# A gated attention and ternary feed-forward block: attention first in a step, exponentials last, work moved from VectorE to ScalarE and GpSimd

## The reference

```python
x = x + jnp.tanh(g_xattn[0]) * _L0_xattn_ref(_layernorm(x, axis=-1), ctx_1024, ctx_1024, ...)
x = x + jnp.tanh(g_ffn[0]) * _L0_ffn_ref(_layernorm(x, axis=-1), w_gate, w_up, w_down)
# one head of the attention: ig, fg are gates of the token, from q, k and v
cs = concatenate([0, cumsum(log_sigmoid(fg))])
log_D = where(lower_triangle, (cs - cs.T)[1:, 1:], -inf) + ig.T
D = exp(log_D - max_log_D)
C = (q @ (k.T / sqrt(DH))) * D
h = C / (maximum(abs(C.sum(-1)), exp(-max_log_D)) + EPS) @ v      # then an RMS norm per head
# the feed-forward half: activations rounded to 8 bits per token, weights to -1, 0, 1
g = act_quant(x) @ weight_quant(w_gate).T
u = act_quant(x) @ weight_quant(w_up).T
h = square(relu(g)) * u
out = act_quant(h) @ weight_quant(w_down).T
```

## Time and profile before

| | |
|---|---|
| median of 3 runs | 704.64 us (703.66 to 706.67) |
| the profiled execution | 707.75 us, of it the span of the core 706.0 us |
| TensorE busy | 602.2 us (85%), granted clock 0.944 of full speed on average |
| VectorE busy | 568.5 us (81%) |
| ScalarE busy | 424.0 us (60%) |
| GpSimd busy | 97.9 us (14%) |
| HBM traffic | 63.73 MB, mean 90 GB/s |

### The profile page before, as it was taken

How to read it: one execution, slowest core, us unless ns; L and a number is a source line. 1 busy time by engine, 2 the same in 40 slices (tenths; PEclk the granted TensorE clock), 3 DMA queues, 4 the chain that set the end, 5 groups by cost and what they waited for, 6 DMA issues and landing times.

```text
span 706.0 us, 18248 instructions
## 1 busy us (share of the span) xinstructions
PE 602.2 (85%) x6596; PEld 347.4 (49%) x6596; DVE 568.5 (81%) x1288; ACT 424.0 (60%) x893; POOL 97.9 (14%) x170
## 2 busy tenths in 40 slices
PE   7384776989989898998989898989989898989887
PEld 4151433545545454554646454555546464556443
DVE  4388559797879879697988979797979889797965
ACT  4376894657466465757556565657466565666542
POOL 1165020101001010101001010101000010101000
PEclk9797888999999999999999999999999999999999
DMA  9945201304040220404040230405040311402000
GB/s 311 381 160 177 85 0 56 127 17 165 3 165 15 97 82 15 164 0 164 15 164 15 64 116 15 164 0 179 0 164 15 108 72 38 144 17 76 2 30 31
DMA packets 45168, 63.73 MB, mean 90 GB/s; under 512 B 1872, under 2 KB 26704, under 8 KB 45136
## 3 DMA queue, kind: packets, MB, share of 16 engines
q1 hardware_dynamic: 43024, 61.19, 24.8%
q10 hardware_dynamic: 2112, 2.11, 0.9%
HBM read 54.77 MB, written 8.52 MB: 90 GB/s over the span
## 4 chain that ended last, share of the span: by engine, by line
DVE 31%; PE 29%; issue 20%; ACT 12%; DMA 5%; DVEq 1%; POOL 1%; SPq 0%; ACTq 0%; POOLq 0%
PE gb L1032 9%; PE ub L1032 7%; ACT dmat L528 4%; DVE stage L721 4%; PE yb L1055 4%; DVE dmat L824 3%; DVE hmaxes L729 3%; PE ab L1063 3%; DMA dmat<-max_rows 3%; ACT dmat L522 2%; PE tp L1076 2%; DVE ssq L842 2%; DVE amax L883 2%; PE ab L1043 2%; DVE x L865 1%
## 5 line engine op out<-in xcount | busy, mean ns | idle before, releaser
L1032 PE MATMUL gb<-wgT,xqT 128*128 128x512 bf16 x512 | 145.3, 410 | 4.9 <-ACT xqT L509 2.8
L1032 PE MATMUL ub<-wuT,xqT 128*128 128x512 bf16 x512 | 141.9, 403 | 0.9 <-DVE stage L721 0.9
L1055 PE MATMUL yb<-wdT,stage 128*128 128x512 bf16 x512 | 120.6, 379 | 2.0 <-ACT stage L502 1.9
L488 ACT ACTIVATE relu<-gb 128x512 f32<-128x512 f32 x128 | 75.6, 590 | 50.7 <-PE gb L1032 49.7
L721 DVE TENSOR_TENSOR stage<-relu,ub 128x512 f32<-128x512 f32 x128 | 86.7, 681 | 14.3 <-ACT relu L490 13.6
L424 POOL TENSOR_SCALAR_AFFINE_SELECT dmat<-dmat 128x256 f32<-128x256 f32 x128 | 50.1, 416 | 303.4 <-ACT dmat L528 303.4
L824 DVE SCALAR_TENSOR_TENSOR dmat<-ab,dmat 128x384 f32<-128x384 f32 x128 | 65.3, 551 | 26.3 <-POOL dmat L424 19.5
L1032 PEld LDWEIGHTS ub<-wuT,xqT 128*128 128x128 bf16 x512 | 52.4, 104 | 67.6 <-issue 17.2
L1063 PE MATMUL ab<-qT,cT 64*128 64x256 f32 x256 | 59.0, 436 | 29.5 <-DVE dmat L824 29.5
L490 ACT ACTIVATE relu<-relu 128x512 f32<-128x512 f32 x128 | 80.7, 630 | 4.0
L1055 PEld LDWEIGHTS yb<-wdT,stage 128*128 128x128 bf16 x512 | 48.7, 98 | 58.1 <-ACT stage L502 1.8
(11 more groups left out here) (108 smaller groups left out, 802.0 us busy)
## 6 DMA issues: line engine op xcount, KB each, us to landing
dmat<-max_rows SPq DMA_DIRECT2D x14, 1024.0 KB, 5.1
values<-in_ctx_v SPq DMA_DIRECT2D x16, 520.0 KB, 7.5
xs<-in_x SPq DMA_DIRECT2D x16, 512.0 KB, 5.8
cT<-in_ctx_t SPq DMA_DIRECT2D x16, 512.0 KB, 6.8
out<-stage SPq DMA_DIRECT2D x32, 256.0 KB, 2.1
stage<-in_w_gate SPq DMA_DIRECT2D x4, 1024.0 KB, 13.5
stage<-in_w_up SPq DMA_DIRECT2D x4, 1024.0 KB, 17.4
stage<-in_w_down SPq DMA_DIRECT2D x4, 1024.0 KB, 5.6
```

The source lines that it names most:

```text
L488: nc.scalar.activation(relu[:, c % 2, :], gb[c % 2][:, :], ACT.Relu).then_inc(g_free, 1)
L1032: last = nc.tensor.matmul(bank[c % 2][:, :], xqT[par][:, t, d, :], w[:, d, c * CH:(c + 1) * CH], start=(d == 0), stop=(d == KD - 1))
L1055: done = nc.tensor.matmul(yb[:, :], hqT[:, c, :], wdT[:, c, :], start=(c == 0), stop=(c == KF - 1))
```

## The change

Work moves. The first layer norm is applied by ScalarE, as x times rstd plus a shift, which VectorE works out in one small instruction. Of a hidden tile's rounding ScalarE does the upper half (`quantise_high`), and hq has two buffers. Both hidden copies are ScalarE's. The maximum of the first three chunks is stored in a column behind the fourth, so that the second `tensor_reduce` gives the maximum of all and no combine is needed. dq and the token factors dd, dd2, c3 are worked out by GpSimd.

The order changes on all queues. A step begins with the scores and weighings of n between the chunks of tile 0. The front of m is done in its middle, with the running maximum before the second product of tile 1, and the negated maximum and `exp_minus_max` now in the same step, before the last relu and product of tile 1. The exponentials of m's pairs 0 and 1 stand at the end of ScalarE's step, around `quantise_high(b, 1)` and `tokens(n)`, and those of the pairs 2 and 3 at the start of the next one, ahead of its first relu. The down product of the previous tile is no longer split by the scores. On SP's queue `spread_max` comes first, `store(b, 0)` last.

The diff, cut to its core. Of the new `step` functions of GpSimd, ScalarE, VectorE and TensorE (in this order) the new text stands whole and the old is left out; it stands in the kernel above.

```diff
+hq = [sb(f"hq{t}", [P, FF], F16) for t in range(T)]
...
     for b, n, m in STEPS:
+        if n is not None:
+            uses += [("score", n, kd) for kd in range(KD)]
+        if m is not None:
+            uses.append(("column", m, 0))
         if b > 0:
             uses.append(("hidden", b - 1, 1))
-        if n is not None:
-            uses += [("score", n, kd) for kd in range(KD)]
         uses.append(("hidden", b, 0))
...
     def step(b, n, m, par):
+        if m is not None:
+            spread_max(m, par)
         if not at(b, 0):
             store(b - 1, 1)
-        store(b, 0)
-        if m is not None:
-            spread_max(m, par)
         if m is not None and not at(m, LAST):
             load(m + 1, 1 - par)
+        store(b, 0)
...
+    def token_factor(n, npar):
+        gp.wait_ge(ln2_step, LN2_K * n + 10)
+        alone(gp, gp_passed)
+        nc.gpsimd.tensor_scalar(dd[:, :], am2[:, :], 1.0 / 127.0, 0.0, ALU.mult, ALU.add).then_inc(token_scale, 1)
...
+        nc.gpsimd.tensor_tensor(c3[npar][:, :], dd2[:, :], dd[:, :], ALU.mult).then_inc(c3_ready, 1)
+    def hidden_factor(b, t):
+        gp.wait_ge(quant_step, QUANT_K * (2 * b + t) + 3)
+        if at(b, 0) and t == 0:
+            gp.wait_ge(winv_step, WINV[2] + 1)
+        alone(gp, gp_passed)
+        nc.gpsimd.tensor_scalar(dq[:, t:t + 1], hm1[:, t:t + 1], wprod[:, 2:3], 0.0, ALU.mult, ALU.add).then_inc(dq_ready, 1)
...
     def step(b, n, m, par):
+        if n is not None:
+            masks(n, 2)
+            masks(n, 3)
         if at(b, 0):
             scale_weight(2, 0)
             scale_weight(2, 1)
+        hidden_factor(b, 0)
+        if n is not None:
+            residual(n, 1 - par)
+            token_factor(n, 1 - par)
+        hidden_factor(b, 1)
+        if m is not None:
+            masks(m, 0)
+            masks(m, 1)
...
+        for e in range(2):
+            act.wait_ge(a_full[e], hidden_use(b, t) + 1)
+            nc.scalar.activation(hqT[:, e * KF // 2:(e + 1) * KF // 2, :], abh[e].rearrange("p (k s) -> p k s", s=P), ACT.Copy,
+                                 bias=-MAGIC16).then_inc(a_free[e], 1)
+    def quantise_high(b, t):
+        act.wait_ge(quant_step, QUANT_K * (2 * b + t) + 5)
+        nc.scalar.activation(hq[t][:, FF // 2:], h[t][:, FF // 2:FF], ACT.Copy, scale=hqs[:, t:t + 1],
+                             bias=MAGIC16).then_inc(hq_high, 1)
...
+    def attention_norm(m, par):
+        act.wait_ge(shift_ready, m + 1)
+        for t in range(T):
+            nc.scalar.activation(q[:, t, :], xs[par][:, t, :], ACT.Identity, scale=rstd[:, t:t + 1],
+                                 bias=shift[:, t:t + 1]).then_inc(q_ready, 1)
...
     def step(b, n, m, par):
         npar = 1 - par
         prev = not at(b, 0)
         third = at(b, 0)
+        if n is not None:
+            exponentials(n, 2, npar)
+            exponentials(n, 3, npar)
         relu_square(b, 0, 0)
+        if n is not None:
+            heads(n, 0)
         if third:
             magnitudes(2, 0, 4)
+        relu_square(b, 0, 1)
+        if m is not None:
+            attention_rstd(m)
+        if n is not None:
+            heads(n, 1)
+        if third:
+            magnitudes(2, 1, 5)
+        if m is not None:
+            attention_norm(m, par)
+        relu_square(b, 0, 2)
+        if n is not None:
+            heads(n, 2)
+            heads(n, 3)
+        if m is not None:
+            for t in range(T):
+                columns(m, qT[par], t)
+        relu_square(b, 0, 3)
+        if n is not None:
+            squares(n)
         if prev:
             hidden_cols(b - 1, 1)
         if third:
             magnitudes(2, 2, 6)
             magnitudes(2, 3, 7)
+        if m is not None:
+            forget_gate(m)
+        if n is not None:
+            head_rms(n)
+        quantise_high(b, 0)
         relu_square(b, 1, 0)
         if third:
             scale_weight(2, 2)
             scale_weight(2, 3)
             sign_weight(2, 0, 4)
+        relu_square(b, 1, 1)
+        if n is not None:
+            tokens_rstd(n)
+        hidden_cols(b, 0)
+        if third:
             sign_weight(2, 1, 4)
+        relu_square(b, 1, 2)
+        if n is not None:
+            quantise_second(n)
+        if m is not None:
+            exp_minus_max(m, par)
         if third:
             sign_weight(2, 2, 4)
             sign_weight(2, 3, 4)
         relu_square(b, 1, 3)
+        if m is not None:
+            exponentials(m, 0, par)
+        quantise_high(b, 1)
         if n is not None:
             tokens(n, npar)
+        if m is not None:
+            exponentials(m, 1, par)
...
+        if part == 0:
+            dve.wait_ge(h_done, 8 * b + 4 * t + 3)
+            nc.vector.tensor_reduce(h[t][:, FF:FF + 1], h[t][:, 0:3 * CH], axis=AX_X, op=ALU.max,
+                                    apply_absolute_value=True).then_inc(quant_step, 1)
...
+            nc.vector.tensor_reduce(hmax[:, t:t + 1], h[t][:, 3 * CH:FF + 1], axis=AX_X, op=ALU.max,
+                                    apply_absolute_value=True).then_inc(quant_step, 1)
...
+    def quantise_low(b, t):
+        dve.wait_ge(quant_step, QUANT_K * (2 * b + t) + 5)
+        nc.vector.tensor_scalar(hq[t][:, 0:FF // 2], h[t][:, 0:FF // 2], hqs[:, t:t + 1], MAGIC16,
+                                ALU.mult, ALU.add).then_inc(quant_step, 1)
...
+    def attention_shift(m):
+        nc.vector.scalar_tensor_tensor(shift[:, :], mv[:, :, 0], -1.0, rstd[:, :], ALU.mult, ALU.mult).then_inc(shift_ready, 1)
...
     def step(b, n, m, par):
         npar = 1 - par
         prev = not at(b, 0)
         if n is not None:
             weigh(n, 0)
             weigh(n, 1)
+        hidden(b, 0, 0)
         if n is not None:
             weigh(n, 2)
             weigh(n, 3)
         if m is not None:
+            attention_stats(m, par)
+        hidden(b, 0, 1)
         if n is not None:
             weigh(n, 4)
             weigh(n, 5)
+        if m is not None:
+            attention_shift(m)
         if n is not None:
             weigh(n, 6)
             weigh(n, 7)
+        hidden(b, 0, 2)
+        hidden_max(b, 0, 0)
+        if n is not None:
+            normaliser(n, npar)
+        hidden(b, 0, 3)
+        if n is not None:
+            head_squares(n)
+        if m is not None:
+            gates_in(m)
+        hidden_max(b, 0, 1)
+        if m is not None:
+            log_forget(m)
         if not prev:
             weight_scale(2)
             dve.wait_ge(winv_step, WINV[2])
             nc.vector.scalar_tensor_tensor(wprod[:, 2:3], wmean[:, 2:3], 1.0 / 127.0, tanhs[:, 1:2],
                                            ALU.mult, ALU.mult).then_inc(winv_step, 1)
+        hidden_scale(b, 0, par)
+        quantise_low(b, 0)
+        if n is not None:
+            scale_heads(n)
+        if m is not None:
+            cumulative(m, par)
+        if prev:
+            output(b - 1, 1, npar)
+        if n is not None:
+            residual(n, npar)
         hidden(b, 1, 0)
         if n is not None:
+            token_stats(n, npar)
+        if m is not None:
+            running_max(m, par)
+        if n is not None:
+            token_centres(n, npar)
         hidden(b, 1, 1)
         if n is not None:
+            quantise_tokens(n)
         hidden(b, 1, 2)
         hidden_max(b, 1, 0)
         if m is not None:
+            negated_max(m)
         hidden(b, 1, 3)
+        hidden_max(b, 1, 1)
+        hidden_scale(b, 1, par)
+        quantise_low(b, 1)
+        output(b, 0, par)
...
-            pe.wait_ge(quant_step, QUANT_K * (2 * b + t) + QUANT_K - 2 + e)
+            if e == 0:
+                pe.wait_ge(quant_step, QUANT_K * (2 * b + t + 1))
+            else:
+                pe.wait_ge(hq_high, 2 * b + t + 1)
...
     def step(b, n, m, par):
         npar = 1 - par
         prev = not at(b, 0)
         if n is not None:
             scores(n, 0, npar)
             scores(n, 1, npar)
+        chunk(b, 0, 0, par)
         if n is not None:
             scores(n, 2, npar)
             scores(n, 3, npar)
             heads_out(n, 0, npar)
+        chunk(b, 0, 1, par)
+        if n is not None:
             scores(n, 4, npar)
             scores(n, 5, npar)
             heads_out(n, 1, npar)
             scores(n, 6, npar)
             scores(n, 7, npar)
+        chunk(b, 0, 2, par)
+        if n is not None:
             heads_out(n, 2, npar)
+        if m is not None:
+            q_columns(m, par)
+        if n is not None:
+            heads_out(n, 3, npar)
+        chunk(b, 0, 3, par)
+        if prev:
+            hidden_transposes(b - 1, 1)
+        else:
+            weight_total(2)
+        if m is not None:
+            gate_products(m, par, 0, 2 * T * KD)
+        if prev:
+            down(b - 1, 1, 0, KF)
+        if m is not None:
+            cumulative_sum(m)
         chunk(b, 1, 0, par)
+        if m is not None:
+            a_rows(m, par)
         chunk(b, 1, 1, par)
```

(4 more changed lines are left out.)

225 lines of the change are left out of this document (65 added, 160 removed).

## The result

The changed kernel takes 741.97 us (median of 4 runs, 740.7 to 742.63); the kernel before, on the same chip, 704.27 (703.66 to 706.67). The ratio is 1.052, 95% interval 1.049 to 1.055: slower by 37.7 us, where 18.4 were forecast. The two profiled executions, 741.91 and 707.75, differ by 34.2: the one of the kernel before lay 3.5 above the median of its runs, and the traces account for the 34.2. All times are in us.

A forecast was written before the change was run, and what follows sets the result against it. The prediction took VectorE's work as the bound, TensorE 1 to 3 us behind; 12 steady intervals at 41.2 against 39.74 gave +17.5, the first interval and ends +0.9, so +18.4 and 723 us, range 684 to 744.

The forecast's parts named there:

- (a): Step's start, from R00 (relu and square of chunk 0, token tile 0) through weighings to chunk 2's start: 6.9 us.
- (b): TensorE's part of the step, from chunk and heads through the down product to tile 1's first product: sum 15.5 us.
- (c): VectorE's part, through token statistics and maxima, with R13 waiting behind exp_minus_max: sum 11.2 us.
- (d): Step's end: last chunk's maximum, rounding, token copies and three pairs of exponentials before the next R00: sum 7.6 us.
- the clock, priced at 0: TensorE at 1.2 GHz at the turn: scores and chunk 0 take 2.6 more, hidden by R00's 2.5 of slack.
- rule against row: After idle at the turn, the skill's rule has half clock in every step, the measured rows only in some.
- The first interval and the ends: First interval, start and last steps outside the 12 steady intervals: together +0.9 us, bounds -5 and +6.
- The first: Rival, faster: layout's waits for R13 and R00 do not add up; step 36.0, time 661 to 683; chance 0.28.
- The second: Rival, clock: down product at half clock in most steps, longer waits for scores; +20 more, 743; chance 0.15.
- The third: Rival, balance: shorter VectorE queue and new waits meet within a per cent of 704, layout 3% too long; chance 0.10.
- The fourth: Rival: transfer of the maxima late by a microsecond; +12 more, 735, within the forecast's own range; no separate chance.
- What the prediction said to look for: Profile signs: VectorE busy under 30, ScalarE near 30, stores 41.2 apart, named waits present, no wait for x.

The follow-up runs named there:

- experiment 1: The changed kernel with exp_minus_max put behind the last relu of tile 1 instead of ahead of it: 725.86 us, ratio 1.029 to the kernel before.
- 3: The changed kernel with the token copies ahead of the upper rounding of tile 1 on ScalarE: 724.88 us, ratio 1.028 to the kernel before.
- 6: The changed kernel with exp_minus_max behind the last relu and the token copies ahead of the upper rounding: 709.07 us, ratio 1.007 to the kernel before.
- experiment 7: The mended order: the changed kernel's work, with token copies, exp_minus_max, first relus, squares and running maximum reordered: 678.63 us, ratio 0.964 to the kernel before.
- experiment 5: The changed kernel with 14 idle matmuls behind the token transposes to keep TensorE busy at the turn: 741.96 us, ratio 1.054 to the kernel before.
- Experiments 9 to 12: The mended order with work returned to VectorE: upper rounding (9, 675.96 us); plus layer norm (10, 674.59), plus second hidden copies (11, 688.66), plus both (12, 688.12).
- Experiment 4: The kernel before, in its own order, with the change's roundings, norms, copies and small instructions moved: 732.72 us, ratio 1.039 to the kernel before.
- 2: The changed kernel with the step's first relu, R00, ahead of the exponentials of pairs 2 and 3: 747.01 us, ratio 1.059 to the kernel before.
- experiment 8: The changed kernel with exp_minus_max late, token copies ahead of the upper rounding and R00 ahead of exponential pairs 2 and 3: 692.87 us, ratio 0.981.

## Why the prediction was right in its sign and short in its size

**The layout of the cycle held.** From R00 at 337.01 to the next at 378.33 it is 41.32, forecast 41.2. By its pieces, with the starts in the trace after: (a) 7.2 to chunk 2's start at 344.18, forecast 6.9; (b) 15.2 to the product at 359.35, forecast 15.5; (c) 11.4 to the last maximum at 370.76, forecast 11.2; (d) 7.6, forecast 7.6. The waits are those named: 3.1 for R00 (3.7 forecast), 1.6 for R02 (1.7), 1.4 for R13 (1.5), 1.2 for R03 (1.3), and 4.2 of TensorE at scores 0, where 3.7 stood. The down product's wait for its copy is 0.90 in that step (1.1). Experiments 1, 3, 6 and 7 show that these waits, and not the loads, are the main cause: the same work in another order is 63 us faster.

Three smaller numbers of the working do not come out. The terms printed in (b) add up to 15.2, which is what was measured; 0.3 of its 15.5 has no term. ScalarE's load was given as 28.5, but 24.18 and the moved pieces at the prices named make 29.6, and 29.55 was measured. VectorE's busy time was to fall by 5.1 to 28.6 and fell by 3.7 to 29.97; the 30.0 taken for its queue hid this. None of the three enters the 41.2 by more than 0.3.

**The steps: +25.7, not +17.5.** The term of the sum that failed here is the clock, priced at 0. First, the sum set a step laid out at the full clock, 41.2, against 39.74, and this average has the slow steps of the kernel before in it. Its steps with the clock at 1.00 take 38.2, so at equal clock the new order costs 3.1 a step and not 1.5; the slow steps cost the kernel before 1.5 a step on average. Secondly, the change has slow steps as well. The prediction said "R00 has 2.5 of slack behind the exponentials". R00 has it, but what follows has not. Where the half clock reaches all of chunk 0's second product (1.91 at 418.99), scores 2 and R01 are late, and it is 42.6 from this R00 to the next. Where the product takes 1.65 (at 294.38) it is 41.9, and where it takes 1.24 or 1.03 (at 336.18 and 377.59) it is 41.3 or 41.4. The twelve intervals are 41.88 on average, so this is about 0.55 a step, 7 us. The size lies within the +10 that the prediction allowed the clock, but the place is another: it named the down product, and in the steady steps its sixteen matmuls took 3.62 where all are recorded, no longer than in the rows before (3.61). The rest, 0.1 a step, is within the rounding of the layout.

On rule against row, the trace after decides: at every turn of its steady steps chunk 0's first product ran at half clock (1.82 to 1.89 for four matmuls, 1.48 or 1.49 for three, where 1.04 and 0.81 are usual), behind a wait of 4.0 to 4.2. What differs from step to step is how far into chunk 0 it lasted. The Trainium skill's "TensorE: Matmul & The Clock Gate" (Part 1: The HAM clock gate) has half rate as the resting state, which only activity lifts. The trace agrees: the new turn brings the lower clock in every step.

**The first interval and the ends: +8.4, not +0.9.** This term was the worse miss in proportion, and its bounds of -5 and +6 do not hold it. It also does not follow from its own parts: 2.8 for the exponentials, -1 and +2 for the start and the last steps, and between 0 and 4.0 for the down weights make +3.8 to +7.8, since the 8.4 of the running maximum only moves time from before the first store to behind the last. By these parts the first store should come 9.4 earlier and came 14.9 earlier, and the tail should grow by 10.4 and grew by 14.0. Of the tail, 3.1 go in experiment 5 (81.6 and not 84.7, at a mean clock of 0.99 and not 0.96 there), so that part probably is the clock again; the rest was not separated and stays open.

**Work and order.** "By loads alone a step could fall to about 35. What decides is the order" was right for the change. The prices of the moved work were good for the rounding (1.15 busy and 1.05 between starts, as taken) and the copies (1.01), and too low for the norm (0.81 each, 0.59 to 0.72 taken). But the prediction counted 4.6 us as leaving VectorE's queue and nowhere said which of it stood on the path. Experiments 9 to 12 answer this: in the mended order the copies pay their 1.16 a step, the norm nothing, and the rounding costs 0.27. Experiment 4 shows that in before's order the moves together, as placed there, lose 28 us. The change's own order takes another 9 from that, and the mended one turns it into a gain of 26, or 30 with the rounding given back.

What this gain consists of can be worked out from the steps, though no run separates it. Experiment 7 saves 2.07 in each interval against the kernel before. Of these, 1.5 are the slow steps, which it does not have, and 0.55 is a shorter step at equal clock (37.67 against 38.22). The clock is thus a small part of what the change lost and a large part of what the mended order wins.

**The rivals.** The first, that the waits do not add up, is wrong for the change: they stand in full. Its price for their absence, 661 to 683, holds what experiment 7 reached with most of the waits removed, 678.6, though with a step of 37.67 and not 36.0. The second is wrong as the main cause (experiment 5) and right as about half a microsecond a step. The third had the cycle 3% too long, and it was not. The fourth, the transfer late, did not happen in the change but did in experiment 1. What the prediction said to look for was seen: the two waits for x that are left, 6.5 us of 23.5, both lie in the first 9 us of the span, and in the steps there is none. That the measured time lies inside the range of 684 to 744, close to its upper end, owes something to the width of that range: the two terms that failed add up to 15.7 us, nearly as much as the 18.4 forecast.

Open: how much of experiment 7's gain each of its edits has beyond those of 1, 2 and 3. From 8 to 7 there are 12 to 14 us for splitting the pairs of exponentials and the hidden copies, the token copies ahead of pair 0, and the earlier running maximum together. Of the last the traces show that the wait for the transfer of the maxima, some 0.6 a step in experiment 8, is gone in 7.

## What to carry to other kernels

Before work is moved off a busy engine, mark where on its queue it has no gap and where it waits anyway. In this kernel only work of the first kind paid when it was moved (the copies), and not all of it: the upper rounding of tile 0 stood in such a stretch too, but ScalarE, which took it, had no time to spare at the turn for that of tile 1. In a queue that is worked in order, put first what another engine waits for (here the token copies before a rounding), and put nothing that waits for a late value ahead of something ready. A step laid out with measured durations came out right to some tenths here. The ends of the pipeline need the same care as the step, and a step of one kernel should be compared with a step of the other at the same clock. A fix that seems to fail alone may be worth 16 us once the wait ahead of it is gone.
